# POOL waits for the landing of each indirect DMA before it issues the next, in routing and experts

## The reference

```python
x = x + _L0_attn_a_ref(_layernorm(x), ...)
x = x + _L0_ffn_ref(_layernorm(x), ...)
x = x + _L0_attn_b_ref(_layernorm(x), ...)
x = x + _L0_ffn_ref(_layernorm(x), ...)

def _L0_ffn_ref(x, sw1, sw2, sw3, ew1, ew2, ew3, rw, rb):
    shared = (silu(x @ sw1) * (x @ sw2)) @ sw3
    probs = softmax(x @ rw + rb)                 # 8 experts
    w, idx = top_k(probs, 2); w = w / sum(w)     # 2 experts for each token
    routed = sum over the two: w * ((silu(x @ ew1[e]) * (x @ ew2[e])) @ ew3[e])
    return shared + routed
```

## Time and profile before

| what | value |
|---|---|
| time, median of 3 runs | 1792.38 us (1787.33 to 1798.26) |
| span of the profiled execution | 1895.4 us |
| first to last scatter of ffn1r (from 755.84 us), and of ffn2r | 97 us, 102 us |
| first to last indirect DMA of ffn1e, and of ffn2e | 132 us, 137 us |
| indirect DMAs: ahead 16, ffn1r 48, ffn1e 80, ffn2r 64, ffn2e 80 | 288 |

### The profile page before, as it was taken

The page is one execution under the profiler, slowest core; times in us unless marked ns, Lnnn a source line. Parts: engine busy times, 40 slices in busy tenths (PEclk is TensorE's granted clock), DMA queues, the critical chain, the costliest instruction groups (busy, mean ns, idle before and its releaser), DMA issues. The chain is left out here.

```text
span 1895.4 us, 27842 instructions
## 1 busy us (share of the span) xinstructions
PE 1386.3 (73%) x8207; PEld 690.9 (36%) x8208; DVE 1268.0 (67%) x2981; ACT 845.2 (45%) x1215; POOL 881.2 (46%) x775
## 2 busy tenths in 40 slices
PE   4359999999999888766885776775865445546882
PEld 1113333333333555445773221321311003335772
DVE  4666999999983576643332498999989995533333
ACT  3404666666667332213442776484573321112441
POOL 3401121121212645753554169788696664652552
PEclk9756999999999899878997887886986666878996
DMA  4721111211120331622224578959758636114225
GB/s 131 238 79 41 54 53 44 62 47 52 57 64 16 101 103 47 180 65 80 78 72 121 156 164 207 231 131 246 181 156 215 162 99 165 62 62 121 79 75 150
DMA packets 218312, 210.68 MB, mean 111 GB/s; under 512 B 49247, under 2 KB 188482, under 8 KB 215874
## 3 DMA queue, kind: packets, MB, share of 16 engines
q1 hardware_dynamic: 196174, 180.70, 35.8%
q0 software_dynamic: 9216, 19.02, 3.1%
q10 hardware_dynamic: 12800, 9.46, 1.6%
HBM read 145.27 MB, written 63.37 MB: 110 GB/s over the span
## 5 line engine op out<-in xcount | busy, mean ns | idle before, releaser
L804 ACT ACTIVATE attn_prob<-attn_ps_cols 128x1024 f32<-128x1024 f32 (+1 forms) x320 | 292.1, 940 | 219.5 <-PE attn_ps_cols L680 218.5
L2534 POOL TENSOR_TENSOR ssm_hc<-ssm_h,ssm_cb 128x1024 f32<-128x1024 f32 x128 | 300.6, 2356 | 135.2 <-DVE ssm_h L2517 111.1
L2517 DVE TENSOR_TENSOR_SCAN ssm_h<-ssm_decay,ssm_ps_u 128x1024 f32<-128x1024 f32 x128 | 292.7, 2286 | 29.9 <-ACT ssm_decay L2505 13.7
L830 POOL TENSOR_SCALAR_AFFINE_SELECT attn_prob<-attn_prob 128x512 f32<-128x512 f32 x128 | 81.2, 634 | 415.7 <-ACT attn_prob L804 415.7
L712 DVE CUSTOM_DVE_ANT_0 attn_ps_rows<-attn_ps_rows,const_mask_rows 128x384 f32<-128x384 f32 (+3 forms) x512 | 236.0, 520 | 39.7 <-PE attn_ps_rows L647 37.5
L647 PE MATMUL attn_ps_rows<-attn_ks,attn_qs 72*128 72x512 bf16 (+3 forms) x768 | 228.4, 351 | 44.4 <-DMA attn_qs<-parts_dram 31.2
L2505 ACT ACTIVATE ssm_decay<-ssm_wide,ssm_aneg 128x1024 f32<-128x1024 f32 x128 | 146.1, 1146 | 174.4 <-DVE ssm_h L2517 96.3
L2468 PE MATMUL ssm_ps_u<-ssm_stack,ssm_spread 96*128 96x512 bf16 x256 | 95.9, 465 | 155.3 <-DVE ssm_h L2517 148.5
L680 PE MATMUL attn_ps_cols<-attn_qs,attn_ks 75*128 75x512 bf16 (+3 forms) x768 | 194.3, 333 | 4.7 <-DMA attn_qs<-attn_nrows 4.1
L699 PE MATMUL attn_ps_o<-attn_prob,attn_vw 128*32 128x512 f32 (+3 forms) x1536 | 166.6, 506 | 0.3 <-POOL attn_prob L830 0.3
L717 DVE TENSOR_REDUCE attn_nm<-attn_ps_rows 128x1 f32<-128x512 f32 x256 | 157.8, 681 | 7.8 <-PE attn_ps_rows L647 7.7
(11 more groups left out here) (361 smaller groups left out, 2491.9 us busy)
## 6 DMA issues: line engine op xcount, KB each, us to landing
ssm_wide<-delta_dram SPq DMA_DIRECT2D x128, 512.0 KB, 6.7
attn_ks<-parts_dram SPq DMA_DIRECT2D x48, 192.0 KB
attn_qs<-parts_dram SPq DMA_DIRECT2D x48, 192.0 KB
parts_dram<-proj_parts SPq DMA_DIRECT2D x8, 768.0 KB, 3.8
ffn1e_x<-ex_dram SPq DMA_DIRECT2D x40, 130.0 KB
ffn2e_x<-ex_dram SPq DMA_DIRECT2D x40, 130.0 KB
split_dram<-ssm_parts SPq DMA_DIRECT2D x6, 768.0 KB, 4.4
ssm_stack<-split_dram SPq DMA_DIRECT2D x18, 256.0 KB, 4.3
```

The source lines that it names most:

```text
L804: nc.scalar.activation(prob[u % RING][:, heads[0]:heads[-1] + 1, 0:w], ps_cols[s % 2][:].rearrange("p b (x q) -> p (b x) q", x=len(heads) ...
L2517: nc.vector.tensor_tensor_scan(h[t % H_RING][:], decay[t % DECAY_RING][:], ps_u[t % 2][:], 0.0, ALU.mult, ALU.add).then_inc(scan_done, 1)
L2534: nc.gpsimd.tensor_tensor(hc[:, t % HC_RING, :], h[t % H_RING][:], cb[b % 2][:], ALU.mult).then_inc(hc_done, 1)
```

## The change

In front of every indirect DMA POOL now also waits until the indirect DMA that it issued before it in the same stage (in the first routing: before it in the list of scatters, from the memory stage on) has landed, that is, until its semaphore `sent` has all 16 counts of it. The first of each list has nothing to wait for. The rings, the order of POOL's instructions, the DMAs and the other engines' programs stay as they were.

```diff
--- scatter (routing)
         pool.wait_ge(r.pos_ready, u + 1)
+        pool.sem_inc(r.passed, 1)
+    before = u * TOP * UPT + j - 1
+    if before >= 0:
+        v, at = before // (TOP * UPT), before % (TOP * UPT)
+        pool.wait_ge(r.sent[v % DEEP], (v // DEEP * TOP * UPT + at + 1) * 16)
         pool.sem_inc(r.passed, 1)
     n, j = j // UPT, j % UPT
     nc.gpsimd.indirect_dma_start(dram["ex"], bass.IndirectOffsetOnAxis(ap=r.pos[k][:, n, j:j + 1], axis=0),
--- run_experts, POOL
                         pool.wait_ge(out_ready, now(s * SUB + (j + 1)))
+                        if j:
+                            pool.wait_ge(sent[q], now(i * (SUB * 16) + j * 16))
+                        elif past(s, 1):
+                            ui, uq = shifted(i, q, -1)
+                            pool.wait_ge(sent[uq], now(ui * (SUB * 16) + SUB * 16))
                         pool.sem_inc(passed, 1)
                         nc.gpsimd.indirect_dma_start(dram["ey"], bass.IndirectOffsetOnAxis(ap=x[q][:, j, TOKEN:TOKEN + 1].bitcast(I32), axis=0),
```

## The result

The kernel after takes 2327.5 us (2317.8 to 2332.0) against 1795.3 us (1787.3 to 1801.6) on the same chip: a ratio of 1.297, 95% interval 1.292 to 1.302. The forecast was 2178 us with a range to 2270: right in its sign, 150 us too low. The profiled execution of after took 2332.0 us.

What follows compares the result with a forecast made beforehand. The prediction took PE to set the pace in the expert stages and no engine to be full in routing. Its terms, 8.3 + 74.4 + 71.7 + 116.5 + 115 = 386 us, on 1792.4 gave 2178 us, range 2035 to 2270.

Steps and rivals of the forecast that it cites:

- memory stage: Unit 0 of ffn1: eighth scatter 21.0 us after the first, its mask late and uncovered; +8.3 us, between 0.6 and 12.5.
- ffn1r: First routing stage: unit 1 slowed by the weight load (+16 us), then 47 intervals of 3.0 us; +74.4 us in all.
- ffn1e: First expert stage: POOL becomes the bound at 6.3 us a tile, 79 x 3.15 = 248.9 us against 132.4; +116.5 us.
- ffn2r: Second routing stage: 64 scatters 3.0 us apart plus a 3.4 us tail, normalisation hidden under them; +71.7 us.
- I carry the difference over as it is: Baseline step: the profiled span's 103 us above the unprofiled median kept unchanged, so 1792.4 + 386 = 2178 us.
- P: Price of one waited indirect DMA, start to start: 3.0 us (3.15 in the experts), bounds 2.2 to 3.6, where 1.26 was possible.
- Piece 1: Start of an indirect DMA to its landing with semaphore: between 1.9 and 2.6 us, taken as 2.2.
- Piece 2: Release of POOL's wait to the start of the next indirect DMA: 0.81 or 0.98 us in rows, taken as 0.8.
- Dear landing: Rival: other transfers meet more indirect DMAs than counted, price 3.4 us or more, 2262 up to 2345 us; chance 0.13.
- Cheap restart: Rival: part of the 0.8 us passes while the landing is awaited, price 2.5 us, 2039 us; chance 0.17.
- Not slower: Rival: the wait ends within today's 0.30 us gap, price stays 1.26 us, time stays 1792 us; chance 0.03.
- both short: Rival: dispatch nearly free and landing 2.2 us, price 2.2 us, 1955 us; chance 0.05.

Runs made afterwards that it cites:

- e1: The kernel before, unchanged, profiled once more: 1796.2 us, ratio 1.000, span 1794.5 us.
- e2: The kernel after with only the waits in front of the scatters, the experts as before: 2044.0 us, 1.139 of the kernel before.
- e8: The kernel after with waits only at the scatters of units 0 and 1 of ffn1: 1828.3 us, 1.019 of the kernel before.
- e9: The kernel after plus a waited half-size indirect DMA in front of each of the experts' 160: 2801.8 us, 1.560 of the kernel before.
- e3: The kernel after with only the waits at the experts' indirect DMAs, the routing as before: 2079.0 us, 1.158 of the kernel before.
- e6: The kernel after with each scatter's wait carried by its indirect DMA, without the semaphore instruction: 2257.7 us, 1.258 of the kernel before.
- e5: The kernel after with waits moved to landings long past, a unit or two tiles back: 1797.3 us, 1.000 of the kernel before.
- e10: The kernel before with the last wait of a unit's first scatter carried by its indirect DMA: 1795.7 us, ratio 0.999.

## Why the forecast missed

| term, us | forecast | after against the first profile of before | after against e1 |
|---|---|---|---|
| memory stage, to its end | 8.3 | 17.3 | 17.2 |
| ffn1r, to the first load of ffn1e | 74.4 | 90.5 | 110.7 |
| ffn1e, to the first instruction of ssm | 116.5 | 117.2 | 138.2 |
| ssm | 0 | 5.8 | 5.6 |
| ffn2r, to the first load of ffn2e | 71.7 | 88.8 | 122.1 |
| ffn2e, to the join | 115 | 115.7 | 141.3 |
| rest | 0 | -0.5 | 0.6 |
| sum | 386 | 434.8 | 535.7 |

**The step that failed first: "I carry the difference over as it is".** The forecast had the span 103 us above the median, said that no row tells where these lie, and added the change's cost to the median. That holds only if the 103 us outlive the change. They did not: they went with waits of ACT and DVE for late counts of PE in the four stages in which POOL becomes the bound, so that POOL's chain decides the time there, and the kernel after had no such waits in any case. The last two columns differ by 101 us. Rows did tell: the "remote" waits, and that PE, called the pace of the experts, was busy for only 112.8 of 134 us. From first to last e1's scatters of units 2 and on take 62.4 us in ffn1r, 84.3 in ffn2r, and the indirect DMAs of an expert stage 111.5. Set against these, with the same prices, the terms are 8.3 (memory stage), 16 + 141 - 62.4 = 94.6 (ffn1r), 248.9 - 111.5 = 137.4 (ffn1e), 189 - 84.3 = 104.7 (ffn2r) and 137.4 + 3 = 140.4 (ffn2e), together 485 us: 2278 us. The claim that PE would hide a price of up to 1.71 us falls with it: at 2.85 us a tile it hides up to 1.42. (One bound of the prediction is a slip: for the memory stage it takes 0.6 us at P = 1.9, under its own lower bound of P, 2.2.)

**The terms that were too small**, the other 50 us. In the experts the price was right: 250.1 and 252.9 us from first to last, where 248.9 was forecast (3.17 and 3.20 for 3.15 us each). In the routing it was 3.22 and 3.28 for 3.0. Piece 1, "I take 2.2", is 2.30 in the scatters (median) and 2.4 to 2.5 in the mean, since some landings meet other transfers: in ffn2r 49 with under 0.005 MB of other packets beside them take 2.30 us in the mean, and 11 that meet 0.05 MB or more take 3.23 (the longest idle there was 7.7 us). So 47 and 63 intervals took 151.3 and 206.8 us instead of 141 and 189, together 28 us. Piece 2, 0.8 us, is right to 0.01. Under the weight load unit 1 took 43.4 us to the first scatter of unit 2 instead of 38.0. The memory stage is 17.2 us longer instead of 8.3; POOL's rows there in the kernel after:

```profile
726.28 1.23 POOL L1555 DMA_INDIRECT ex_dram<-ahead_xn,ahead_pos  x1 [0.19 <-issue]
730.81 0.96 POOL L1555 DMA_INDIRECT ex_dram<-ahead_xn,ahead_pos  x1 [3.31 <-DMA ex_dram<-ahead_xn,ahead_pos]
...
751.18 0.96 POOL L1555 DMA_INDIRECT ex_dram<-ahead_xn,ahead_pos  x1 [2.38 <-ACT mem_raw L1230]
752.17 2.49 POOL L1285 TENSOR_TENSOR mem_am<-mem_raw,const_strict 128x512 f32<-128x512 f32 x2
```

The eighth scatter starts 24.9 us after the first, not 21.0: some starts are 4.5 us apart. Of the 17.2 us 3.4 lie in front of the stage's first scatter, where nothing has waited yet (108.2 us into the stage, 104.8 in e1). With the same edit the stage is 11.3 us longer in e2, 10.2 in e8 and 10.7 in e9: the change costs it some 10 to 14 us, and the rest varies from one execution to the next. The 5.6 us of ssm, where nothing was changed, are 3.4 in e3 and absent in e6 (566.2 us against e1's 565.7), whose experts are those of after; the runs do not tie them to the change, and their cause is open.

**What was right.** The two pieces, the sign, POOL as the bound of all four stages, the zero stores and DVE's normalisation hidden under the scatters, the duration of 0.96 us. The tail from the last scatter to the first load of ffn2e, forecast at 3.4 us, is 2038.42 - 2034.88 = 3.5 in the kernel after:

```profile
2034.88 0.96 POOL L1555 DMA_INDIRECT ex_dram<-ffn2r_xn,ffn2r_pos  x1 [2.19 <-DMA ex_dram<-ffn2r_xn,ffn2r_pos]
...
2038.42 6.16 SPq L1909 DMA_DIRECT2D ffn2e_x<-ex_dram  x6
```

**The rivals.** "Dear landing" gave the nearest time (2262 to 2345 us), but by luck: the terms in which landings meet other transfers came out 42 us larger (28 in the routing, 9 in the memory stage, 3.4 of them in front of any wait, 5 in unit 1), not 84, and most of the distance is the baseline. "Cheap restart" is false for this change and true in e6: with the wait on the DMA itself P is 2.56 us (median), close to its 2.5, and the argument against it rests on waits that, by the kernel's code, also sit on an instruction of their own; no run moved those that end last. "Not slower" and "both short" are out, by periods of 3.0 us and more.

The Trainium skill, "DMA: Bandwidth & Descriptors", section "Anatomy of one DMA — SWDGE (gpsimd) path", has a fixed 2.0 us and bytes behind it: e9 agrees that the fixed part is nearly all of it, and the landing of 2.25 to 2.30 us is near the 2.15 that the prediction estimated from it. Its 50 ns of dispatch are shown by no run here; the shortest step from landing to start is the 0.27 us of e6. The Trainium skill, "Perfetto Trace Analysis", section "DMA Instruction — SWDGE (GPSIMD)", says that such an instruction's end is that of descriptor writing and not of the transfer. The traces agree that it is not that of the transfer: the instruction ends 0.96 us after its start, its landing is counted 1.3 us later.

## What to carry to other kernels

A wait for the landing of the DMA just issued costs landing plus restart for each DMA, nearly the same for 64 rows as for 128, as soon as no other engine is slower than that sum; waits for landings a tile or a unit further back cost nothing that shows (e5). Let the DMA itself carry the wait where the wait is not met already (0.54 us each in e6, nothing in e10). Where the profiled execution is longer than the timed ones, find the stages that hold the excess first, and take neither cover nor pace from them: where a change makes another engine the bound, the stage's new length is that engine's chain, the excess is no part of it, and the cost against an undisturbed execution is larger than the rows say.

## What the hardware showed unexpectedly

A scatter behind a semaphore instruction that waits starts 0.81 us after the last count; one that waits itself starts 0.27 us after it. Half the rows of an indirect DMA save 0.06 us of POOL's 0.96. In one execution of the kernel before, ACT and DVE got counts of PE 2 to 14 us after the recorded end of the matmuls (waits of 125 us in all); in e1, the same kernel, they did not.
